# A two-layer AdaLN/FFN kernel: w's loads on another queue, narrow expert masks spread by a product, a last slot in chunks, a new order of work

## What is computed

```python
ekv_t, ek_t = swap(exp(k) * v), swap(exp(k))
nf, df = scan(a*decay + ekv_t), scan(b*decay + ek_t)        # forward, and the same backward: nb, db
num = nf + nb - ekv + euk * vf
den = df + db - ek + euk
out = sigmoid(r) * num / max(den, 1e-8) * (0.8 + 0.2 * tf)  # r = x

# layer 0
prob = softmax(xf @ Wg.T); gate = argmax(prob)
h = einsum('nd,erd->ner', xf, A) * one_hot(gate)[:, :, None]
x = x + einsum('ner,eor->no', h, Bw) * 4 * prob[gate]
# layer 1
h = gelu(x @ quant(w1).T + b1)          # quant: sign where |w| >= 0.7 * mean|w|, else 0
x = x + h @ quant(w2).T + b2
```

## Time and profile before

| | us |
|---|---|
| runs | 101.97, 103.10, 103.27; median 103.1 |
| the profiled execution, its own time | 102.21 |
| its span, first to last instruction | 100.4 |
| PE busy in the span | 89.8 (89%) |
| DVE busy | 86.5 (86%) |
| ACT busy | 79.9 (80%) |
| POOL busy | 66.3 (66%) |
| granted PE clock, mean | 1.00 |

### The profile page before, as it was taken

One profiled execution on the slowest core, in us unless ns is written; L12 is line 12 of the kernel. 1 busy time (PEld: TensorE's weight loads), 2 busy tenths in 40 slices (PEclk: granted clock), 3 DMA queues, 4 the chain that ended last, 5 costly groups with the idle time before them and its releaser, 6 DMA issues. The chain is left out here.

```text
span 100.4 us, 2070 instructions
## 1 busy us (share of the span) xinstructions
PE 89.8 (89%) x633; PEld 80.9 (81%) x633; DVE 86.5 (86%) x203; ACT 79.9 (80%) x144; POOL 66.3 (66%) x90
## 2 busy tenths in 40 slices
PE   3897669989978999999799999999899999799980
PEld 2686549977777888888588888889799999699970
DVE  2479999999999999999999999999999997983330
ACT  4279999999986769999766589997997899976520
POOL 4067679979985697059769897999982967005310
PEclk9999999999999999999999999999999999999999
DMA  1889999700000000000000000000000021100005
GB/s 20 258 262 320 308 245 378 313 3 0 3 0 0 3 0 7 0 0 0 0 3 0 7 0 0 0 0 0 0 0 7 0 104 70 35 0 10 0 0 209
DMA packets 6886, 6.43 MB, mean 64 GB/s; under 512 B 2370, under 2 KB 6492, under 8 KB 6876
## 3 DMA queue, kind: packets, MB, share of 16 engines
q1 hardware_dynamic: 6868, 6.31, 20.1%
q10 hardware_dynamic: 8, 0.00, 0.0%
HBM read 5.26 MB, written 1.05 MB: 63 GB/s over the span
## 5 line engine op out<-in xcount | busy, mean ns | idle before, releaser
L298 POOL TENSOR_TENSOR h_lo<-h,h_hi 128x512 fp32r<-128x512 f32 x9 | 12.3, 1373 | 12.0 <-DVE h_hi L306 7.0
L794 DVE TENSOR_TENSOR_SCAN run<-bank,kv 128x256 f32<-128x256 f32 x32 | 20.0, 670 | 0.1
L1224 PE MATMUL bank<-xin_hi,w1T 128*128 128x256 f32 x64 | 15.8, 287 | 0.9 <-DVE xin_lo L292 0.5
L1156 PE MATMUL bank<-num,AT 128*128 128x256 f32 x64 | 15.5, 384 | 0.7 <-DVE hm L900 0.5
L1258 PE MATMUL bank<-w2T,h_hi 128*128 128x256 f32 x64 | 16.1, 288 | 0.0
L1258 PE MATMUL bank<-w2T,h_lo 128*128 128x256 f32 x64 | 15.6, 281 | 0.0
L611 ACT ACTIVATE h<-bank,bT 128x256 f32<-128x256 f32 x32 | 13.3, 478 | 2.8 <-PE bank L1224 2.6
L1224 PE MATMUL bank<-xin_lo,w1T 128*128 128x256 f32 x64 | 15.2, 278 | 0.0
L1172 PE MATMUL bank<-hm,BT 128*128 128x256 f32 x64 | 14.6, 382 | 0.1
L1224 PEld LDWEIGHTS bank<-xin_hi,w1T 128*128 128x128 f32 x64 | 12.0, 188 | 1.8 <-DVE xin_lo L292 0.8
L1156 PEld LDWEIGHTS bank<-num,AT 128*128 128x128 f32 x64 | 11.6, 190 | 2.2 <-issue 0.9
(11 more groups left out here) (141 smaller groups left out, 216.5 us busy)
## 6 DMA issues: line engine op xcount, KB each, us to landing
w_nat<-in_L_ffn_w_dram SPq DMA_DIRECT2D x2, 1024.0 KB, 8.3
F_nat<-in_fside_BxSxS_dram SPq DMA_DIRECT2D x4, 256.0 KB, 3.5
x_nat<-in_x_dram SPq DMA_DIRECT2D x4, 256.0 KB, 4.9
out_dram<-outb SPq DMA_DIRECT2D x3, 256.0 KB, 2.1
A_nat<-in_L_ffn_A_dram SPq DMA_DIRECT2D x1, 512.0 KB, 5.8
B_nat<-in_L_ffn_Bw_dram SPq DMA_DIRECT2D x2, 256.0 KB, 6.6
out_dram<-outb SPq DMA_DIRECT2D x2, 128.0 KB, 1.9
wv_rows<-in_L_cond_w_dram SPq DMA_DIRECT2D x2, 1.0 KB
```

Source lines behind the costliest of these rows:

```text
L298: eng.tensor_tensor(h_lo[:, b % 2, 2 * j:2 * j + 2], h32[:, b % 2, 2 * j:2 * j + 2], h_hi[:, b % 2, 2 * j:2 * j + 2].bitcast(F32), ALU.sub ...
L794: dve.tensor_tensor_scan(run[:, r, c, q], decay_ps[:, l, c, b:b + 1].broadcast_to([P, T]), kv[:, b, c, q], 0.0, ALU.mult, ALU.add).then_in ...
L1156: mm = pe.matmul(bank[H_BANK + k][:, (m % 2) * T:(m % 2 + 1) * T], AT[:, c, m * P:(m + 1) * P], num_at(0, b)[:, c], start=(c == 0), stop=( ...
L1224: mm = pe.matmul(bank[g_bank[g]][:, (f % 2) * T:(f % 2 + 1) * T], w1T[:, c, f * P:(f + 1) * P], part[:, b % 2, c], start=(c == 0 and part ...
```

## The change

Six things change. *w* is loaded by two transfers on ACT's queue behind `cond`; its two exponentials are taken on the rows as loaded (4 partitions x 128), ahead of the first keys' exponential, and PE's transpose follows them, which DVE's `decays` reads from the PSUM bank. *The expert masks* are 8 columns wide (`hot`), one for each expert. PE transposes them to 8 rows, ACT copies these (`copy_hot`), and a product with the constant `spread` (8 x 128, ones where column // 16 is the row) makes the 128 rows; `copy_mask` follows as before. `gate_reciprocal` is a step of its own. *The last slot* (layer 1, block 3) has its denominator in two banks, and from `backward_last_chunk` on each channel chunk is a step of its own: addition, logarithm, exponential, products, `last_xin_high`, `last_xin_low`; `last_hidden(j, c)` multiplies one chunk. *The last quarter of h* goes in two halves through GELU, split and product (`last_gelu`, `last_h_high`, `last_h_low`, `last_ffn_out`). Some steps change engine: `times_values(0)`, `add_num(1, 2)` and three more `seed` to DVE, `clip_keys(1)`, `times_tanh(2)` to POOL, `xin_high(1)` to ACT, two `h_low` to DVE. And *all lists have a new order*, with 10 and 16 `keep_warm` and four `warm_up`. The cut diff (lines cut away are other semaphore names, the small hunks around `decays` and the free-bank rules, and parts of the lists):

```diff
-        mask = sb("mask", [P, 2 * NT, P])
+        hot = sb("hot", [P, 2 * NT, NE])
+        hot_rows = sb("hot_rows", [NE, 2, T])
...
-        g_bank = [7, 4] * 4 + [6, 7, 4] * 2 + [6, 7]
+        g_bank = [7, 4] * 4 + [6, 7, 4] * 2 + [6, 2]
...
+        LL, LB = LAYERS - 1, NB - 1
+        LR, LU = ring(LL, LB)
+
+        def last_den(c):
+            return bank[den_bank[NB * LL + LB - c]][:, 0:T]
...
             load_F(0)
-            for k, v in enumerate((w_l0, w_l1)):
-                sp.dma_start(wv_rows[NC * k:NC * (k + 1), :], v.rearrange("(c p) -> c p", p=P)).then_inc(wv_loaded, 16)
             load_F(1)
             for k, v in enumerate((u_l0, u_l1)):
...
-                pool.memset(expert_of[:, e * P // NE:(e + 1) * P // NE], float(e)).then_inc(consts_ready, 1)
+                pool.memset(expert_of[:, e:e + 1], float(e)).then_inc(consts_ready, 1)
+
+            pool.memset(spread[:, :], 1.0).then_inc(consts_ready, 1)
+            pool.wait_ge(consts_ready, 5 + NE)
+            pool.affine_select(out=spread[:, :], in_=spread[:, :], compare_op=ALU.is_ge, fill=0.0, base=0,
+                               pattern=[[1, P]], channel_multiplier=-(P // NE)).then_inc(consts_ready, 1)
+            pool.wait_ge(consts_ready, 6 + NE)
+            pool.affine_select(out=spread[:, :], in_=spread[:, :], compare_op=ALU.is_ge, fill=0.0, base=P // NE - 1,
+                               pattern=[[-1, P]], channel_multiplier=P // NE).then_inc(consts_ready, 1)
...
             gains()
-            times_values(pool, 0)
+            seed(pool, 0, 0, DEN)
             factors()
-            seed(pool, 0, 0, DEN)
-            seed(pool, 0, 1, DEN)
+            clip_keys(pool, 1)
             seed(pool, 0, 0, NUM)
             times_values(pool, 1)
             own_values(pool, 0, 0)
-            clip_keys(pool, 2)
             add_num(pool, 0, 0)
             times_sigmoid(pool, 0)
+            seed(pool, 0, 1, DEN)
+            num_times_rec(0, 0)
+            clip_keys(pool, 2)
+            seed(pool, 0, 1, NUM)
+            times_values(pool, 2)
             own_values(pool, 0, 1)
-            seed(pool, 0, 1, NUM)
-            num_times_rec(0, 0)
             add_num(pool, 0, 1)
+            times_sigmoid(pool, 1)
+            clip_keys(pool, 3)
+            num_times_rec(0, 1)
...
         def _(act):
             act.dma_start(cond_rows[:, :], cond).then_inc(cond_loaded, 16)
+            for k, v in enumerate((w_l0, w_l1)):
+                act.dma_start(wv_rows[NC * k:NC * (k + 1), :], v.rearrange("(c p) -> c p", p=P)).then_inc(wv_loaded, 16)
             act.preload_act_table_set("natural_log_exp_and_others")
 
             def decay_exps():
-                act.wait_ge(front_psum, 2)
-                act.activation(edecay[:, :], bank[MISC_BANK][:, VEC_AT:VEC_AT + LAYERS * NC], ACT.Exp).then_inc(edecay_ready, 1)
+
+                act.wait_ge(wv_loaded, 16 * LAYERS)
+                act.activation(wv_rows[:, :], wv_rows[:, :], ACT.Exp).then_inc(edecay_ready, 1)
                 act.wait_ge(edecay_ready, 1)
-                act.activation(edecay[:, :], edecay[:, :], ACT.Exp, scale=-1.0).then_inc(edecay_ready, 1)
+                act.activation(wv_rows[:, :], wv_rows[:, :], ACT.Exp, scale=-1.0).then_inc(edecay_ready, 1)
...
+            def last_log_den(c):
+                act.wait_ge(den_ready[LR], LU + c + 1)
+                act.activation(run[:, LR, c, DEN, :], last_den(c), ACT.Ln, scale=LN_SCALE).then_inc(ln_done[LR], 1)
+
+            def last_reciprocal(c):
+                act.wait_ge(ln_done[LR], LU + c + 1)
+                act.activation(run[:, LR, c, DEN, :], run[:, LR, c, DEN, :], ACT.Exp, scale=-1.0, bias=recip_bias[:, 0:1]).then_inc(rec_ready[LR], 1)
...
+
+            def copy_hot(b):
+                act.wait_ge(hot_psum, b + 1)
+                act.activation(hot_rows[:, b % 2], bank[MISC_BANK][0:NE, MASK_AT:MASK_AT + T], ACT.Copy).then_inc(hot_copied, 1)
...
             cond_exp()
+            decay_exps()
             first_key_exp(0)
-            decay_exps()
             first_key_exp(1)
+            first_scaled_values()
             key_exp(1)
-            first_scaled_values()
             u_exps()
             act.preload_act_table_set("sigmoid_and_others")
             sigmoid(0)
             scaled_values(1)
+            scaled_values(2)
             sigmoid(1)
-            scaled_values(2)
             sigmoid(2)
             sigmoid(3)
             act.preload_act_table_set("natural_log_exp_and_others")
+            log_den(0, 0)
+            evacuate_A(0)
+            reciprocal(0, 0)
             key_exp(2)
-            evacuate_A(0)
+            evacuate_A(1)
+            key_exp(3)
+            evacuate_B(0)
             scaled_values(3)
-            key_exp(3)
+            evacuate_B(1)
             evacuate_Wg()
-            evacuate_B(0)
-            log_den(0, 0)
-            evacuate_A(1)
-            reciprocal(0, 0)
+            abs_sum(0)
             log_den(0, 1)
-            abs_sum(0)
+            gate_exp(0)
+            reciprocal(0, 1)
             abs_sum(1)
-            evacuate_B(1)
-            reciprocal(0, 1)
-            gate_exp(0)
+            copy_hot(0)
+            copy_mask(0)
             sign_below(0)
             sign_above(0)
-            copy_mask(0)
+            log_den(0, 2)
...
             gelus(2, 0)
+            h_high(act, 2, 0)
+            gelus(2, 1)
             act.preload_act_table_set("natural_log_exp_and_others")
-            log_den(1, 3)
-            reciprocal(1, 3)
+            last_log_den(0)
+            last_log_den(1)
+            last_reciprocal(0)
+            last_reciprocal(1)
+            act.preload_act_table_set("gelu_and_others")
+            gelus(2, 2)
             result(act, 1)
-            act.preload_act_table_set("gelu_and_others")
-            gelus(2, 1)
-            h_high(act, 2, 1)
-            gelus(2, 2)
+            h_high(act, 2, 2)
             gelus(2, 3)
             gelus(3, 0)
             gelus(3, 1)
+            h_high(act, 3, 1)
             gelus(3, 2)
             h_high(act, 3, 2)
-            gelus(3, 3)
-            h_high(act, 3, 3)
-            result(act, 2)
+            last_gelu(6)
+            last_gelu(7)
+            last_result(act, 0)
...
+            def backward_last_chunk(c):
+                dve.wait_ge(fwd_steps[DEN][LR], (NC + 1) * (LU + 1))
+                if c == 0:
+                    den_bank_free(LL, LB)
+                else:
+
+                    dve.wait_ge(ratio_ready[NB * LL + LB - 1], 1)
+                dve.tensor_tensor_scan(last_den(c)[:, ::-1], decay_ps[:, LL, c, LB:LB + 1].broadcast_to([P, T]),
+                                       run[:, LR, c, DEN, ::-1], 0.0, ALU.mult, ALU.add).then_inc(bwd_done[DEN][LR], 1)
...
+            def last_product(c):
+                dve.wait_ge(q_ready[LR], LU + c + 1)
+                wait_numerator(dve, LL, LB)
+                dve.tensor_tensor(sig[:, LB, c], last_den(c), num_at(LL, LB)[:, c], ALU.mult).then_inc(ratio_ready[NB * LL + LB], 1)
...
-                    dve.tensor_scalar(mask[:, i % (2 * NT)], expert_ps, bank[DVE_BANK][:, IDX_AT + i:IDX_AT + i + 1],
+                    dve.tensor_scalar(hot[:, i % (2 * NT)], expert_ps, bank[DVE_BANK][:, IDX_AT + i:IDX_AT + i + 1],
...
             forward_chunk(0, 0, DEN, 1)
-            clip_keys(dve, 1)
+            times_values(dve, 0)
             inverse_gains()
-            forward(0, 1, DEN)
             forward(0, 0, NUM)
             place_factors()
             backward(0, 0, DEN)
             own_keys(0, 0)
             backward(0, 0, NUM)
+            add_den(0, 0)
+            forward(0, 1, DEN)
+            forward(0, 1, NUM)
+            den_times_rec(0, 0)
+            backward(0, 1, DEN)
             own_keys(0, 1)
-            add_den(0, 0)
-            backward(0, 1, DEN)
-            forward(0, 1, NUM)
+            ratio(0, 0)
             add_den(0, 1)
+            backward(0, 1, NUM)
+            gate(0)
+            forward(0, 2, NUM)
+            gate_reciprocal(0)
+            gate_index(0)
+            own_keys(0, 2)
+            expert_mask(0)
+            den_times_rec(0, 1)
             forward(0, 2, DEN)
-            den_times_rec(0, 0)
-            backward(0, 1, NUM)
-            ratio(0, 0)
-            own_keys(0, 3)
-            own_keys(0, 2)
-            gate(0)
+            ratio(0, 1)
             thresholds()
-            gate_index(0)
+            select_expert(0, 1)
             backward(0, 2, DEN)
-            den_times_rec(0, 1)
-            expert_mask(0)
-            ratio(0, 1)
-            forward(0, 2, NUM)
-            forward(0, 3, DEN)
-            select_expert(0, 1)
-            gate(1)
             select_expert(0, 0)
             add_den(0, 2)
             backward(0, 2, NUM)
+            gate(1)
+            forward(1, 0, DEN)
             gate_index(1)
+            forward(0, 3, DEN)
+            gate_reciprocal(1)
```

(122 more changed lines are left out.)

283 lines of the change are left out of this document (158 added, 125 removed).

## The result

The changed kernel takes 106.59 us (median of 4 runs, 105.3 to 108.11), the kernel before 103.19: ratio 1.034, 95% interval 1.026 to 1.043. It is slower by 3.4%; 100.6 us was forecast. The profiled execution took 106.78 us, its span is 105.0 us, and TensorE's work ends at 101.8 us where the walk had 94.3.

What follows compares the result with a forecast made beforehand. VectorE was taken to set the pace until the last denominator, TensorE the end. TensorE's end 3.1 us earlier, less 0.6 for jitter, gave -2.5 us: 100.6 us instead of 103.1, range 98.9 to 102.8.

Steps and rivals of the forecast that it cites:

- the walk: Durations added step by step through the engines' queues; without the 0.6 us added for jitter, TensorE ends at 94.3 us.
- Front: Loads and exponentials before the first scan: w on ScalarE's queue brings that scan 0.35 us earlier, from 5.69 us.
- The first gate: First scan to end of ratio(0, 0): 12.9 us on VectorE, so TensorE starts at 18.4 us instead of 21.42.
- VectorE's load up to the last denominator: VectorE's list up to the last slot's denominator: 1.65 us less, with the front complete at 79.0 instead of 81.03 us.
- The mask path: Narrow masks from compare to selection: about 1.2 us more latency a block, hidden, tightest at block 0 with 0.25 us margin.
- The rival: Mask rows come late and VectorE stands at select_expert in each block: 108 us, chance 0.05; milder, 103 to 105, 0.05.
- one sign: The mask stall rival's example price per block: VectorE waits for one ScalarE sign step, 1.99 us, in four blocks.
- TensorE's clock: Rival: fewer fillers and warm-ups halve TensorE's rate, expert products take 3 us more, 103.6 us, over 106 if lasting; chance 0.03.
- Tail: Behind the last denominator: chunk 0's low part ready at 84.35 us, chunk 1's at 85.8, against 86.80 before.
- TensorE's remainder: TensorE's work after the last xin_lo: six half hidden and six ffn_out, 8.45 us instead of 10.6.
- TensorE's idle: Rival: TensorE's idle time stays at 3.5 us and takes half the gain, 102.1 us; chance 0.30 for 101.0 to 103.

Runs made afterwards that it cites:

- e12: e3 with w's two rows loaded by SyncE's queue behind F(0), as in the kernel before; 101.68 us, 0.987 of the kernel before.
- e1: Changed kernel with 19 filler transposes of the identity in TensorE's gaps between 23.5 and 28.6 us, spread_mask(0) moved ahead of weight_totals; 106.15 us.
- e2: Changed kernel with four VectorE steps set apart from POOL's: second threshold read from PSUM, own_keys(1, 3) earlier, two POOL h_low waiting; 102.97 us.
- e4: Changed kernel with masks 128 columns wide again, without the narrow copy and the spreading product; 107.23 us, 1.042 of the kernel before.
- e3: The repaired kernel: changed kernel with the edits of both e1 and e2; 101.00 us, 0.988 of the kernel before.
- e6: Changed kernel with own_keys(1, 3) ahead of h_low(0, 3) and add_num(1, 2), POOL's last two h_low made to wait; 103.39 us, 1.008 of the kernel before.
- e8: Kernel before with early fillers keep_warm cut from 19 and 27 to 10 and 16, nothing else; 102.98 us, 1.000 of the kernel before.
- e7: e3 with its last slot whole again instead of in halves; 102.46 us, 1.002 of the kernel before.
- e11: e3 with masks 128 columns wide again, without the narrow copy and the spreading product; 102.85 us, 0.999 of the kernel before.
- e10: e3 with filler transposes in TensorE's first gap alone (7, 0 and 0 instead of 7, 6 and 6); 102.57 us.

## Why the prediction was wrong

**Front.** First scan 5.97 instead of 5.35: within the bounds (5.1 to 6.1), but later than before where it was to be earlier, because w's transfer behind cond's on ScalarE's queue landed at 4.47. I had taken it to be hidden by the table load that ends near 3.7. e12 puts the price at 0.66, from one pair of executions; by the spread of the others it is 0.2 to 0.9.

**The first gate.** 12.9 us from first scan to the end of `ratio(0, 0)` were forecast, 12.85 measured (5.97 to 18.82). `gate_logits` at 18.88 instead of 18.4. Right in this execution, and so is that POOL and ScalarE are not late. In e1, e2, e4 and e12 ScalarE's reciprocal was late, by 0.85 to 3.2 us of wait on VectorE: A's copy stands ahead of the reciprocal and waits for TensorE's transposes of A, and the walk has no term for these.

**VectorE's load up to the last denominator.** This step failed. 79.0 was forecast, 84.02 came. In the repaired kernel it is 80.17, so the list itself was short by 1.2 us: the gate was 0.3 late, there is a gap of issue of 0.35 ahead of `forward(0, 2, NUM)`, and the compares, 287 ns each, save 1.0 us (4 x 0.25) where I had 1.85; the rest of the list came out 0.3 better than its sum (it has two more seeds on VectorE, as counted, not three as written under "The change"). The other 3.9 us are in no row of the list. I wrote that the sum "holds only if VectorE never starves" and then asked only whether its inputs come in time. Starved it was once, for 2.0 us; 1.6 us are steps lengthened by POOL's, which count as busy, and 0.2 is the later gate. The overlap of VectorE's steps with POOL's was put at nothing without a reason: the walk laid the two queues beside each other to find who waits for data, and never asked which steps run at the same time.

**The mask path.** Block 0's rows were in time (no wait at its selections), though later than walked: 26.41 against 25.7, the selection at 27.80 against 25.95. Blocks 2 and 3 too. Block 1, which the text doesn't discuss, was the one that stalled, and not by the path's own length: TensorE ran at 1.2 GHz. The rival had the place of the price right (VectorE at `select_expert`) and its size for one block (2.0 us against "one sign", 1.99), but the size is luck: ScalarE was itself waiting for TensorE (0.92 us ahead of the copy of the narrow rows), and the same instructions made VectorE wait 0.6 us in e6.

**TensorE's clock.** The rival with 3 in 100 is the one that came, mixed with the one above. Its arithmetic was right (3.75 us for what takes 1.9), its reason was weak: I reasoned that 1.62 of 3 us busy at a clock of 1.00 meant safety. The changed kernel fell after 1.77 of 3. e8 shows a fall with fewer early fillers that makes VectorE wait for nothing, though most runs of the kernel before have a low stretch somewhere too (means of 0.967 to 0.983), so the fall can't be put down to them alone. e1 and e3 show that in the changed kernel the three gaps at 23.5 to 28.6 us are to blame for 2.1 us.

**Tail.** From last denominator to the last `xin_low`, 6.8 us were forecast and 6.91 came in the repaired kernel; in the changed one 8.90, the pair of `h_low` (2.38 us) and the cast (1.19) being held. That chunks arrive earlier than a whole slot was wrong by 0.34 (e7); that TensorE profits, right, 1.0 us. TensorE's remainder took 8.9 us against 8.45 (87.08 to 95.94, and 92.92 to 101.81).

**TensorE's idle.** I feared the loss there (0.30). In the repaired kernel it is idle for 0.7 us of 77.3 behind the gate: that fear was empty, in part because fillers now stand in its gaps. In the changed kernel it is idle for 4.9 of 82.9 us, but there the loss began on VectorE.

The account at TensorE's end, 101.8 against 94.3: held steps 2.8 in the tail and 0.7 at the threshold, low clock 2.1, front 0.5, the walk's own error 1.35. With the two causes taken away the kernel takes 101.0 us, where 100.6 was forecast. That is no proof of the walk: its own error of 1.35 us at TensorE's end is over half of the 2.5 us that it promised, and the repaired kernel holds transposes and orders that the forecast kernel didn't.

**What stays open.** What TensorE must do in its gaps to keep its clock. In the profiled executions 1.62 of 3 us busy kept it in the kernel before, 2.00 (24 to 27 us in e11) and 2.29 (e10) kept it, 1.77, 2.01 (e8) and 2.02 (e11) were followed by the fall; and e10's other runs suggest that the same list of instructions does both. What sets the length of the slow stretch at the front, and whether w's queue matters to the end.

## What to carry to other kernels

When an order is changed, lay VectorE's and GpSimd's timelines over each other, step by step: each VectorE step whose operands all lie in SBUF can be held until the end of a GpSimd step, however small it is. Read one operand from PSUM where it costs nothing, or let GpSimd wait where it has time. A schedule that opens gaps of 0.8 to 0.9 us on TensorE several times in a row can pay for them twice; put unneeded transposes there. And judge a repair by marks in two profiles, from one step to the next, before you call it worthless: e1 gained 2.2 us behind the gate while its time hid more than half of that in an unrelated wait ahead of it.

## What the runs showed that was not expected

- A VectorE step on two columns, SBUF to SBUF, took 1.05 us beside a GpSimd step (1.17 in e8), 0.17 in the kernel before, where it began 0.07 us ahead of one. The pair that reads PSUM took 0.15 each.
- The granted clock went to 1.2 GHz after waits of at most 0.94 us (changed kernel), 0.97 (e11) and 1.18 (e8), and stayed there for 3.4 us (e6, e8) to 6.8 us (changed kernel; from the windows' means, what lacks to 1.00 over 0.5, times 3 us), most of it with TensorE fully busy again. The Trainium skill (TensorE: Matmul & The Clock Gate, "The HAM clock gate") says that idling halves the rate; how short the gaps can be is what these runs add.
- How long the clock stays low differs between executions with the same instructions there (VectorE's wait 2.0 us and 0.6).
- TensorE's first transposes run at about half their later rate while the clock column reads 1.00; the stretch ends between 10 and 11 us in the changed kernel's execution and behind 17 us in that of e1, where the first gate opens 1.4 us later.
- w's 1 KB rows were used 0.67 us later by a queue with one small transfer ahead of them (e3) than by one with 256 KB ahead (e12), one execution of each; in e4 the first queue had them as early as the second (3.66 and 3.62).
